# One message product per turn of sixteen tiles, in 256 columns, and both comparisons ahead of sixteen adds

## The chip, the core and the metric

The kernel runs on one core of one Trainium2 chip. The core has five engines: TensorE (PE in the rows, its weight loads PEld), VectorE (DVE), ScalarE (ACT), GpSimd (POOL) and SyncE (SP). The metric is the device time of one launch in microseconds (us). Lower is better.

## What is computed

Seven graph layers run over one graph of 6250 nodes and 106250 edges, each with source, destination, one of 8 relation types and a weight. Nodes have 128 features in float32. Five layers are relational and two are weighted means. The change touches the relational ones alone. Cut to what matters, one is

```python
hs = h[src]                                   # one row of 128 per edge
m = sum over b of coef[etype, b] * (hs @ bases[b])        # = hs @ W[etype]
agg = segment_sum(m, dst, num_segments=h.shape[0])
h = relu(agg + h @ loopw + bias) + h_prev
```

Edges come sorted by destination.

## The kernel before

**Tiles.** Edges are cut into 832 tiles of 128. Since destinations are sorted, the 128 edges of a tile fall into a window of 16 neighbouring nodes. A tile's 128 gathered source rows are multiplied on TensorE with a 128x128 table of zeros and ones (`onehot`), whose 128 columns are 8 relations by 16 nodes of the window. That gives, for each relation and each node of the window, the sum of its source rows. These sums then go through the 8 relation matrices, added up in PSUM, and give the messages of the 16 nodes. So weights are applied after the summing, once per window and not once per edge.

**Turns.** Sixteen tiles (`RING`) make a turn, in two halves of eight (`HALF`, h = 0 and 1), and each half in two quads (q = 0 to 3). A relational layer has 52 turns, five layers have 260. A turn, named k, does this:

- GpSimd (L500 to L509) issues 16 indirect DMAs, one per tile, that gather 128 rows of 512 bytes into the slots of `rows_in`. Eight slots of a half may be filled again once the sums of that half are done: it waits for `summed[1]` before half 0 and for `summed[3]` before half 1.
- VectorE (`turn`, L1020 to L1028) makes the tables. `onehots(h)` is 8 comparisons of 128x128 and waits until the sums of the same half in the turn before have read the old ones. `adds(h)` loads 8 window starts, waits for `messaged[h]`, and adds 8 blocks of 128x16 from PSUM into `acc`. Its order is onehots(1), adds(0), onehots(0) of the next turn, adds(1).
- TensorE (`messages`, L764 to L784) makes for half 0 the eight sums, four into bank SUM[0] and four into SUM[1], waits for their evacuation, and then multiplies with the eight relation matrices W into bank MSG[0], 8 tiles by 16 nodes = 128 columns. The same follows for half 1 into MSG[1]. A quad's bank is free when ScalarE has evacuated the quad before it in that bank. The message product of a half also waits until VectorE has added the half of the turn before (`added`).
- ScalarE (`evacuate`, L582 to L590) copies each quad's bank, 128x512, into `sums`.

An engine works its own instructions in program order. What connects them is semaphores: `gathered` (a DMA has landed), `onehot_ready`, `summed`, `evacuated`, `messaged`, `added`. Between turns stand the steps of a chunk of 512 nodes, 13 per layer, whose turns are all done: VectorE applies the relu and adds the old node values, TensorE transposes, and a layer with a normalisation adds moments and a scaling on VectorE. They are interleaved by `edge_chunks`, which runs the turns that a chunk needs and then one step of its pipeline.

Each float32 matmul of the program stands in the trace as two PE rows and two PEld rows, so x16 is eight matmuls.

## Time and profile before

| | |
|---|---|
| median of 3 runs | 9659.97 us (9652.16 to 9668.2) |
| the profiled execution | 9735.56 us, of which the span 9733.8 us |
| TensorE busy | 5450.5 us (56%) |
| VectorE busy | 3272.6 us (34%) |
| ScalarE busy | 1283.5 us (13%) |
| GpSimd busy | 6642.2 us (68%) |
| granted TensorE clock, mean | 0.668 of full speed |
| rows_in gathers of GpSimd | 4160, in five layers of 52 turns |

The page lists busy time of each engine, the span in 40 slices, DMA queues, the chain of work that ended last, and the costliest groups of instructions. An engine's idle time before a group is put down to what ended it. "remote" stands where the event that ended it is not followed back to one instruction, and "issue" where the engine waited for nothing that the profile shows.

### The profile page before, as it was taken

What the parts mean: (1) busy time and instruction counts of PE and PEld (TensorE: products, weight loads), DVE (VectorE), ACT (ScalarE), POOL (GpSimd) and SP (SyncE); (2) the same over time, 40 slices, a digit from 0 to 9 for tenths busy, and PEclk for the clock granted to TensorE, in tenths of its full rate; (3) what the DMA queues carried; (4) which work ended last, traced back from release to release, by engine and by line L of the source; (5) the groups of instructions that cost most, each with busy time, mean ns of one, the idle gap of its engine ahead of it and who ended that gap; (6) DMA issues with size and microseconds to landing.
All of it is one profiled execution on the core that took longest, in us unless ns stands there. A gap on an engine that the chain in (4) does not pass through costs nothing.

```text
span 9733.8 us, 121762 instructions
## 1 busy us (share of the span) xinstructions
PE 5450.5 (56%) x27756; PEld 4997.4 (51%) x27757; DVE 3272.6 (34%) x16373; ACT 1283.5 (13%) x3064; POOL 6642.2 (68%) x5897
## 2 busy tenths in 40 slices
PE   4444554544454455767767544445444546776775
PEld 4444444444444444666666444444444445666664
DVE  3332333333333333433333333333233334333333
ACT  1100111011101111111111200111101111111112
POOL 5666656666566665888888666665666666888887
PEclk7777777677767776555555677777777775555556
DMA  2222221111111111555555511111111114555556
GB/s 92 68 67 67 68 55 45 46 46 46 46 44 45 45 47 45 81 74 74 74 76 74 105 44 46 46 46 46 43 45 45 47 45 73 74 75 76 74 74 114
DMA packets 578875, 595.00 MB, mean 61 GB/s; under 512 B 128465, under 2 KB 470718, under 8 KB 578494
## 3 DMA queue, kind: packets, MB, share of 16 engines
q0 software_dynamic: 373312, 383.17, 23.9%
q1 hardware_dynamic: 170246, 190.65, 6.8%
q10 hardware_dynamic: 35192, 19.90, 0.6%
q14 instruction: 94, 0.77, 0.0%
q8 instruction: 31, 0.51, 0.0%
HBM read 431.39 MB, written 161.82 MB: 61 GB/s over the span
## 4 chain that ended last, share of the span: by engine, by line
another core or an unknown queue 39%; issue 17%; DMA 15%; POOL 13%; PE 8%; ACT 4%; DVE 2%; ACTq 2%; DVEq 1%; SPq 0%; POOLq 0%
DMA share<-scat,place 14%; POOL share L478 13%; PE msg L781 5%; ACT sums L587 4%; PE sum L774 2%; PE lin L726 1%; ACTq L125 1%; DVE acc L980 0%; DVE onehot L967 0%; ACTq L123 0%; ACTq L122 0%; DVE stats L1118 0%; DVEq L967 0%; PE lin L818 0%
## 5 line engine op out<-in xcount | busy, mean ns | idle before, releaser
L509 POOL DMA_INDIRECT rows_in<-h_table,edges_i x3328 | 3171.1, 953 | 1939.9 <-issue 1020.2
L478 POOL DMA_INDIRECT share<-scat,place x1664 | 2601.7, 1564 | 589.9 <-issue 312.8
L781 PE MATMUL msg<-sums,mix_w 128*128 128x128 f32 x4992 | 1137.0, 420 | 1865.8 <-ACT sums L587 1220.1
L781 PEld LDWEIGHTS msg<-sums,mix_w 128*128 128x128 f32 x4992 | 1054.6, 321 | 1927.4 <-issue 1643.1
L980 DVE TENSOR_TENSOR acc<-msg,acc 128x16 f32 x4160 | 729.6, 175 | 3805.3 <-issue 1262.4
L806 PE MATMUL msg<-rows_in,sums 16*128 16x128 f32 x3328 | 1267.4, 482 | 905.7 <-ACT sums L601 904.2
L781 PE MATMUL msg<-sums,rel_w 128*128 128x128 f32 x3328 | 757.0, 419 | 1248.4 <-ACT sums L587 712.7
L806 PEld LDWEIGHTS msg<-rows_in,sums 16*128 16x128 f32 x3328 | 880.7, 322 | 993.3 <-issue 505.8
L781 PEld LDWEIGHTS msg<-sums,rel_w 128*128 128x128 f32 x3328 | 703.6, 322 | 1287.5 <-issue 986.5
L967 DVE TENSOR_SCALAR onehot<-iota_ps,keyT 128x128 f32<-128x128 f32 x4160 | 1166.4, 345 | 477.8 <-issue 442.6
L774 PE MATMUL sum<-onehot,rows_in 128*128 128x128 f32 x8320 | 1262.1, 315 | 73.9 <-issue 46.8
L774 PEld LDWEIGHTS sum<-onehot,rows_in 128*128 128x128 f32 x8320 | 1246.0, 236 | 84.3 <-issue 52.1
L587 ACT ACTIVATE sums<-sum 128x512 f32<-128x512 f32 x1040 | 601.8, 596 | 5211.2 <-remote 3599.9
L509 POOL DMA_INDIRECT rows_in<-in_x_dram,edges_i x832 | 788.6, 948 | 494.7 <-issue 247.5
L808 PEld LDWEIGHTS lin<-ones,sums 16*128 16x128 f32 x3328 | 890.4, 324 | 0.0
L797 PE MATMUL sum<-onehot,near 128*16 128x128 f32 x3328 | 735.6, 415 | 2.5 <-DVE onehot L994 2.5
L808 PE MATMUL lin<-ones,sums 16*128 16x1 f32 x3328 | 693.3, 275 | 0.0
L1006 DVE SCALAR_TENSOR_TENSOR place_f<-repeats,to_spareT 128x8 f32<-128x8 f32 x208 | 35.0, 168 | 1847.1 <-ACT scat L611 1846.1
L797 PEld LDWEIGHTS sum<-onehot,near 128*16 128x16 f32 x3328 | 464.4, 145 | 186.7 <-DVE onehot L994 3.4
L994 DVE TENSOR_SCALAR onehot<-edges_i,srcT 128x128 f32<-128x128 int32 x1664 | 498.4, 312 | 0.0
L607 ACT ACTIVATE place<-place_f 128x4 int32<-128x4 f32 x416 | 85.5, 206 | 2525.9 <-POOLq L477 2511.9
L1000 DVE CUSTOM_DVE_ANT_0 mean<-onehot,before 128x128 f32<-128x128 f32 x1664 | 372.2, 289 | 7.2
(141 smaller groups left out, 2197.3 us busy)
## 6 DMA issues: line engine op xcount, KB each, us to landing
edges_i<-in_src_dram SPq DMA_DIRECT2D x210, 512.0 KB
rows_in<-h_table,edges_i POOLq DMA_INDIRECT x3328
share<-zeros SPq DMA_DIRECT2D x104, 258.0 KB
rows_in<-h_table SPq DMA_DIRECT2D x1664, 8.0 KB
share<-scat,place POOLq DMA_INDIRECT x1664
hT<-share SPq DMA_DIRECT2D x80, 258.0 KB, 4.9
h_table<-rows ACTq DMA_DIRECT2D x65, 256.0 KB
rows_in<-in_x_dram,edges_i POOLq DMA_INDIRECT x832
```

Source lines behind the costliest of these rows:

```text
L478: nc.gpsimd.indirect_dma_start(out=shares[m][a], out_offset=bass.IndirectOffsetOnAxis(ap=place[:, q // 2, 4 * (q % 2) + a:4 * (q % 2) + a ...
L509: nc.gpsimd.indirect_dma_start(out=rows_in[:, s, :], out_offset=None, in_=rows_of[:, :], in_offset=bass.IndirectOffsetOnAxis(ap=srcT_i[:, ...
L587: act.activation(sums[:, h, :, 4 * (q % 2):4 * (q % 2) + 4, :].rearrange("p r t v -> p t r v"), SUM[q % 2][:, :].rearrange("p (t r v) -> p ...
L774: last = nc.tensor.matmul(SUM[q % 2][:, t * KEYS:(t + 1) * KEYS], rows_in[:, 4 * q + t, :], onehot[:, 4 * q + t, :], start=True, stop=True)
L781: last = nc.tensor.matmul(MSG[h][:, 0:HALF * WIN], W[:, n, :], sums[:, h, n, :, :].rearrange("p t v -> p (t v)"), start=(n == 0), stop=(n ...
L797: last = nc.tensor.matmul(SUM[q % 2][0:WIN, t * D:(t + 1) * D], near[:, 4 * q + t, :], same[:, 4 * q + t, :], start=True, stop=True)
L806: nc.tensor.matmul(MSG[q % 2][:, t * D:(t + 1) * D], to_edges, win_rows[:, 4 * q + t, :], start=True, stop=True)
L808: last = nc.tensor.matmul(LIN[q % 2][:, t:t + 1], to_edges, ones[0:WIN, 0:1], start=True, stop=True)
L967: ins = nc.vector.tensor_scalar(onehot[:, slot, :], IOTA[:, 0:KEYS], keyT[:, bass.ds(i * RING + slot, 1)], None, ALU.is_equal)
L980: nc.vector.tensor_tensor(acc[:, at], MSG[h][:, s * WIN:(s + 1) * WIN], acc[:, at], ALU.add).then_inc(added, 1)
L994: ins = nc.vector.tensor_scalar(same[:, slot, :], src_all[:, h, s * D:(s + 1) * D], srcT[:, at], None, ALU.is_equal)
L1000: ins = nc.vector.tensor_tensor_reduce(out=unused[:, s, :], in0=same[:, HALF * h + s, :], in1=before[:, :], scale=1.0, scalar=0.0, op0=ALU ...
```

## The change

It has two parts, both in the turn of a relational layer.

- **One message product.** TensorE now makes the sums of all four quads first and then waits for all four evacuations and for all 16 adds of the turn before. Then it multiplies with the eight relation matrices once, 256 columns wide, into bank MSG[0] alone. `messaged` is one semaphore in place of two. ScalarE, whose evacuation of a half waited for the product of that half in the turn before, now waits for the one product of the turn before.
- **VectorE's order.** onehots(1), onehots(0) of the next turn, adds(0), adds(1). Both halves of adds wait for the one `messaged`, and the second reads columns 128 to 255 of MSG[0].

```diff
@@ scalar: evacuate
-                            act.wait_ge(messaged[h], k + 1)
+                            act.wait_ge(messaged, k + 1)
@@ tensor: start
-            for h in range(2):
-                pe.sem_inc(messaged[h], 1)
+            pe.sem_inc(messaged, 1)
@@ tensor: messages
                                 last.then_inc(summed[q], 1)
-                            for q in (2 * h, 2 * h + 1):
-                                pe.wait_ge(evacuated[q], k + 1 + h)
-                            pe.wait_ge(added, k * RING + HALF * h + HALF)
-                            for n in range(N_RELS):
-                                last = nc.tensor.matmul(MSG[h][:, 0:HALF * WIN], W[:, n, :],
-                                                        sums[:, h, n, :, :].rearrange("p t v -> p (t v)"),
-                                                        start=(n == 0), stop=(n == N_RELS - 1))
-                            last.then_inc(messaged[h], 1)
+                        for q in range(4):
+                            pe.wait_ge(evacuated[q], k + 1 + q // 2)
+                        pe.wait_ge(added, k * RING + RING)
+                        for n in range(N_RELS):
+                            last = nc.tensor.matmul(MSG[0][:, 0:RING * WIN], W[:, n, :],
+                                                    sums[:, :, n, :, :].rearrange("p h t v -> p h (t v)"),
+                                                    start=(n == 0), stop=(n == N_RELS - 1))
+                        last.then_inc(messaged, 1)
@@ vector: adds
-                    dve.wait_ge(messaged[h], k + 2)
+                    dve.wait_ge(messaged, k + 2)
...
-                        nc.vector.tensor_tensor(acc[:, at], MSG[h][:, s * WIN:(s + 1) * WIN], acc[:, at],
+                        nc.vector.tensor_tensor(acc[:, at], MSG[0][:, (HALF * h + s) * WIN:(HALF * h + s + 1) * WIN], acc[:, at],
@@ vector: turn
                         onehots(1, i, k)
-                        adds(0, i, k)
                         with dve.If(i < TURNS - 1):
                             onehots(0, nc.s_assert_within(i + 1, min_val=1, max_val=TURNS - 1,
                                                           skip_runtime_bounds_check_because="the condition above"), k + 1)
+                        adds(0, i, k)
                         adds(1, i, k)
```

TensorE's instructions of one turn stood so before (an x8 is eight matmuls of the program, ISA and REGISTER_ALU are the preparation of waits):

```order
L773 ISA
L774 MATMUL sum<-onehot,rows_in 128x128 x8
L779 ISA
L781 MATMUL msg<-sums,mix_w 128x128 x8
L774 MATMUL sum<-onehot,rows_in 128x128 x8
L778 REGISTER_ALU
L779 REGISTER_ALU
L781 MATMUL msg<-sums,mix_w 128x128 x8
```

and now stand so:

```order
L772 ISA
L773 MATMUL sum<-onehot,rows_in 128x128 x16
L777 REGISTER_ALU
L778 ISA
L780 MATMUL msg<-sums,mix_w 128x256 x8
```

The product of the first half is gone from between the two groups of sums, and the one at the end is twice as wide.

On VectorE, behind the last comparison of onehots(1), stood the loading of the window starts and the first add of half 0:

```order
L967 TENSOR_SCALAR onehot<-iota_ps,keyT 128x128
L973 ISA
L973 TENSOR_LOAD window
L976 REGISTER_ALU
L978 ISA
L980 ISA
L980 TENSOR_TENSOR acc<-msg,acc 128x16
```

and now stands the branch and the comparisons of the next turn's half 0:

```order
L966 TENSOR_SCALAR onehot<-iota_ps,keyT 128x128
L1022 COMPARE_AND_BRANCH
L963 REGISTER_ALU
L966 ISA
L966 TENSOR_SCALAR onehot<-iota_ps,keyT 128x128
```

The adds of half 0 moved behind those comparisons, directly ahead of the adds of half 1, where now stands, between the eighth and the ninth add:

```order
L979 TENSOR_TENSOR acc<-msg,acc 128x16
L972 REGISTER_ALU
L972 TENSOR_LOAD window
L977 REGISTER_ALU
L979 ISA
L979 TENSOR_TENSOR acc<-msg,acc 128x16
```

So all sixteen adds of a turn now stand in one piece, with one loading of window starts inside it.

## Rows read from the trace of the kernel before

**Rows 1.** The page's groups: line engine op, out<-in xcount | busy, mean ns | idle before, releaser.

```profile
L509 POOL DMA_INDIRECT rows_in<-h_table,edges_i x3328 | 3171.1, 953 | 1939.9 <-issue 1020.2
```

**Rows 2.** Groups by line of the stretch 1600 to 2500 us, same columns.

```profile
L509 POOL DMA_INDIRECT rows_in<-h_table,edges_i x597 | 566.2, 948 | 336.5 <-remote 175.1 <-issue 161.1 <-PE sum L774 0.3
L781 PE MATMUL msg<-sums,mix_w 128*128 128x128 f32 x1200 | 276.4, 423 | 448.4 <-ACT sums L587 320.5 <-issue 99.9 <-DVE acc L980 28.0
...
L774 PE MATMUL sum<-onehot,rows_in 128*128 128x128 f32 x1200 | 183.8, 317 | 5.3 <-issue 3.8 <-DMA rows_in<-h_table,edges_i 1.5
...
L967 DVE TENSOR_SCALAR onehot<-iota_ps,keyT 128x128 f32<-128x128 f32 x592 | 166.7, 345 | 71.2 <-issue 66.5
L980 DVE TENSOR_TENSOR acc<-msg,acc 128x16 f32 x599 | 105.1, 175 | 538.3 <-issue 256.6 <-PE msg L781 132.3 <-remote 79.9
```

**Rows 3.** The waits, 1600 to 2500 us: who for whom, us, times, longest.

```profile
ACT sums L587 <- remote: 514.2, 84, 17.4
...
POOL rows_in L509 <- remote: 175.1, 73, 3.9
POOL rows_in L509 <- issue: 161.1, 523, 1.9
```

**Rows 4.** Timeline, one half-turn: start us, us, engine line op, idle before.

```profile
3027.83 0.95 POOL L509 DMA_INDIRECT rows_in<-h_table,edges_i  x1 [2.78 <-remote]
...
3028.33 3.78 PE L781 MATMUL msg<-sums,mix_w 128*128 128x128 f32 x16 [6.21 <-ACT sums L587]
...
3031.89 2.60 PE L774 MATMUL sum<-onehot,rows_in 128*128 128x128 f32 x16
3032.34 2.32 DVE L980 TENSOR_TENSOR acc<-msg,acc 128x16 f32 x8 [2.60 <-PE msg L781]
...
3033.70 0.60 ACT L587 ACTIVATE sums<-sum 128x512 f32<-128x512 f32 x1 [5.61 <-PE sum L774]
...
3036.59 0.95 POOL L509 DMA_INDIRECT rows_in<-h_table,edges_i  x1 [0.30 <-issue]
3039.27 0.60 ACT L587 ACTIVATE sums<-sum 128x512 f32<-128x512 f32 x1 [4.97 <-remote]
3040.04 0.95 POOL L509 DMA_INDIRECT rows_in<-h_table,edges_i  x1 [2.50 <-remote]
...
3040.10 3.65 PE L781 MATMUL msg<-sums,mix_w 128*128 128x128 f32 x16 [5.61 <-ACT sums L587]
```

**Rows 5.** Timeline at the end of layer 1, where GpSimd falls silent after 2570.5 us.

```profile
2556.88 1.06 PE L818 MATMUL lin<-ident,y 128*128 128x128 f32 x4
...
2568.41 2.33 DVE L980 TENSOR_TENSOR acc<-msg,acc 128x16 f32 x8 [16.65 <-remote]
2568.96 1.57 POOL L522 DMA_INDIRECT share<-zeros,lane_i  x1 [0.31 <-issue]
2571.18 0.60 ACT L622 ACTIVATE rows<-lin 128x512 f32<-128x512 f32 x1 [18.10 <-remote]
...
2573.83 2.16 DVE L967 TENSOR_SCALAR onehot<-iota_ps,keyT 128x128 f32<-128x128 f32 x8 [1.47 <-issue]
...
2578.76 2.20 PE L774 MATMUL sum<-onehot,rows_in 128*128 128x128 f32 x16
...
2580.99 0.60 ACT L587 ACTIVATE sums<-sum 128x512 f32<-128x512 f32 x1 [0.23 <-PE sum L774]
```

**Rows 6.** Timeline of a turn in which GpSimd issued sixteen gathers without a pause.

```profile
1503.36 0.95 POOL L509 DMA_INDIRECT rows_in<-h_table,edges_i  x1 [2.65 <-remote]
...
1512.56 2.05 PE L781 MATMUL msg<-sums,mix_w 128*128 128x128 f32 x16 [3.13 <-issue]
...
1522.11 0.95 POOL L509 DMA_INDIRECT rows_in<-h_table,edges_i  x1 [0.30 <-issue]
1526.09 1.08 ACT L587 ACTIVATE sums<-sum 128x512 f32<-128x512 f32 x2 [13.77 <-remote]
...
1526.89 0.95 POOL L509 DMA_INDIRECT rows_in<-h_table,edges_i  x1 [3.83 <-remote]
```

**Rows 7.** Timeline: VectorE's chunk step of a layer with normalisation, first and last group.

```profile
3022.25 0.69 DVE L1102 SCALAR_TENSOR_TENSOR y<-acc,hT 128x512 f32<-128x512 f32 x1 [0.39 <-DVE acc L980]
...
3025.21 1.37 DVE L1144 TENSOR_SCALAR rows<-lin,mv,rstd 128x128 f32<-128x128 f32 x4 [0.15 <-issue]
```

More of the change, by code:

```diff
@@ L275, in build @@
         evacuated = [sem(f"evacuated{q}") for q in range(4)]
-        messaged = [sem(f"messaged{h}") for h in range(2)]
+        messaged = sem("messaged")
         added = sem("added")
```

## The prediction, made before the changed kernel had run

> **What bounds the kernel now.** Read the page's groups first. GpSimd's gathers are the largest, 3171.1 us busy and 1939.9 us idle before them over 3328 of them [rows 1]. That is 1.54 us per gather, 24.6 us per turn of 16, with what lies between layers in it. In a stretch inside a layer there are 597 gathers in 900 us, 1.508 us each, so a turn takes **24.12 us** and a half 12.06 [rows 2]. Of that a gather is 0.948 us busy, and 161.1 us over 523 times is 0.31 us that lies between two gathers whatever happens [rows 3]. Sixteen of them are 16 x 1.25 = 20.0 us. The other 4.1 us of a turn are waits put down to "remote": 175.1 us over 73 times, 2.4 us each, one per half. GpSimd waits there for the sums of the half whose slots it wants to fill.
>
> The timeline of one half shows who makes it wait [rows 4]. GpSimd starts its eight gathers at 3027.83 and issues the last at 3036.59. TensorE's message product runs 3028.33 to 3032.1, and then its eight sums to 3034.5. ScalarE evacuates the first quad at 3033.70, at once. It takes the second only at 3039.27, and GpSimd resumes at 3040.04, 12.21 us after it began. The second quad's sums are recorded as finished 4.8 us before anyone acts on them. No gather is missing: before the sums TensorE is idle for 5.3 us in all of the 900 us [rows 2]. The same shows in the waits, where ScalarE spends 514.2 us waiting for something that the trace can't follow back [rows 3].
>
> Where does that hold of some 5 us come from? Two places of the trace bear on it. At the end of layer 1 TensorE's transposes are recorded until 2557.9, while GpSimd keeps issuing until 2570.5. ScalarE takes their result at 2571.18, 13 us late, and VectorE's adds start at 2568.41 though the product ahead of those transposes was over before 2556.9. Then GpSimd is silent, and the next sums, recorded until 2580.96, are evacuated at 2580.99, with no delay at all [rows 5]. In the other place GpSimd issued 16 gathers from 1503.36 without a pause, the last at 1522.11, and the sums that TensorE had made long before were evacuated at 1526.09 [rows 6]. I read it so: while GpSimd issues gathers, a result of TensorE that comes late in the run of gathers is seen only when GpSimd pauses, and one that comes in the first 4 us of a run is seen at once, as the product is (ended 3032.1, adds at 3032.34 [rows 4]). Why, I can't say. If that is so, the bound is a loop of two: GpSimd pauses for the sums, and the sums are seen because it pauses.
>
> **The change, part by part.** All times below count from T, the moment at which the last quad of a half is seen. GpSimd starts 0.77 us after T (3039.27 to 3040.04) and ends a run of eight at about T + 10.5. The next T is at T + 12.1.
>
> *The product of half 0 goes.* Before, after T of half 0, TensorE did evacuation and start 0.83 us (3039.27 to 3040.10), product 3.65 us, sums 2.0 to 2.6 us: ready at T + 6.5 to 7.1, and held. Now the sums of half 1 need only the evacuations, 2 x 0.60, and 2.6 us: ready at T + 3.8. The 3.65 us are not a gain by themselves, for they lay beside GpSimd's 10 us of issuing. They decide only whether the result falls into the early part of the run.
>
> *The wide product.* At the lower clock the eight matmuls of 128 columns take 3.78 us [rows 4], at the high one 2.05 us [rows 6]. Twice the columns in as many instructions is 4.1 to 7.6 us. Below that, down to one times 2.05, nothing is likely, since the columns are what both numbers scale with. TensorE idles before it as before, so I take the low end of the clock for half of it, 5.9 us. It ends at T + 0.83 + 5.9 = T + 6.7 (4.9 to 8.4), and the sums of the next half 0 follow to T + 8.7 (6.9 to 11.0). Before, that was T + 6.5 to 7.1. Both are ahead of the next T at 12.1, so the 2 us cost nothing. If the hold were gone they would be on the path.
>
> *Halved weight loads.* Their rows overlap the matmuls. I cost them at nothing.
>
> *VectorE's order.* Adds are 2.33 us for eight [rows 5]. Sixteen are 4.7, and the loading of window starts between them about 0.8, since the sequencer can no longer do it behind comparisons (an estimate, half of the 1.47 us that VectorE shows as "issue" before comparisons in [rows 5], where it also went through a loop's end). Then onehots(1) of the next turn takes 2.16 us [rows 5]. Counted from the end of the product: 0.25 + 5.5 + 0.5 + 2.2 = 8.4 us, so T + 15.1 for a product ended at T + 6.7. The sums of half 1 need that table, and they can't start before the next T, T + 12.1, and its two evacuations, T + 13.3. So the table is up to 2 us late for them, they are ready 5 us after the next T, and that still is ahead of the one after it, at 12.1. A chunk step adds 4.3 us (3022.25 to 3026.58 [rows 7]): ready 9.3 us after T, still ahead. VectorE has 65 of these steps and they cost nothing, as long as the product is seen when it ends. New behind the wait for `messaged` are then the eight adds of half 0, onehots(1) and, behind these, the sums of half 1.
>
> *The sum.* With the hold as I read it, two pauses per turn stay and a turn stays at 24.1 us. A gain comes only in turns where the sums of half 1 are ready so early (T + 3.8) that GpSimd needs no pause before half 1. Such a turn lasted 1526.89 - 1503.36 = 23.53 us, 0.6 less [rows 6]. But in it the product then comes late in a run, at about T + 10, is seen only at the pause, and makes the following turn's half 1 late, so every second turn at most: 130 x 0.6 = 78 us. I take a third of the turns, 87 x 0.6 = 50 us, and set against it 30 us for turns in which table or product slip past the pause, an amount between 0 and 65 steps x 1.5 us = 100 us. Forecast: -20 us. The profiled execution is 9735.56 us and would be 9716. The median of the runs is 75.6 us lower, so **9640 us**. The case's own range is 9540 to 9760.
>
> **Rivals.** *The hold belongs to TensorE's sums and not to GpSimd's issuing.* Then it is a fixed 7.2 us from the end of the product to the second quad seen (3032.1 to 3039.27 [rows 4]), twice a turn, and the change takes one product and one evacuation from a chain: 7.2 + 0.6 + 7.2 + 0.8 + (4.1 to 7.6) = 19.9 to 23.4 us. GpSimd can't do a turn under 20.0 + 0.77 = 20.8. So 20.8 to 23.4 against 24.1, that is 180 to 860 us less: 8800 to 9480, middle 9200. For it: the 7.2 us recur in nearly all halves. Against it: in [rows 5] and [rows 6] the hold is 13 and 10 us where GpSimd issues longer, and nil where it is silent. The Trainium skill, SBUF — State Buffer, section "SBUF: two separate sides", says that engine ports and DMA ports can't contend and that TensorE's port waits for nobody. By that rule GpSimd's gathers would not delay sums and this rival would hold, 9200 us. The two places of the trace speak against that reading, but neither shows a port.
>
> *VectorE becomes the link (slower).* If the product, late in a run, is not seen when it ends but at the next pause, then 16 adds, the loading and onehots(1), 8.4 us, start only at T. The table is there at T + 8.4, the sums of half 1 at T + 9.4, at the edge of the run's end at 10.5. With the chunk step's 4.3 us [rows 7] it is T + 13.7. It decides from 12.1 on. That gives 1.6 us or 100 us for 65 steps, and a pause that stretches by up to 1.5 us in each turn gives up to 390 us more: 9760 to 10150, middle 9900. For it: the wide product ends 6 us into a run, where quads are held. Against it: the old product, 4 us in, is seen at once, and a pause ends any hold.
>
> *The change does nothing of what it says.* It removes a wait that lay beside GpSimd's issuing; exactly no effect is 9660, inside my own case.
>
> **Chances.** My case 0.5, the first rival 0.28, the slower rival 0.2, all else 0.02. A measurement of this kernel can tell about 0.2%, 19 us. My case gives 0.2 faster, 0.13 within and 0.17 slower, so with the rivals 0.48 faster, 0.14 same, 0.38 slower. The range must leave out 0.2: downward the deeper part of the first rival (below 9250, some 0.12), upward the tail of the slower one (above 9930, some 0.08).
>
> **What would show it.** In the profile after: GpSimd's waits for "remote" still once per half and about 2.4 us each if I am right, gone or halved if the first rival is. The product's group with 256 columns between 260 and 480 ns per instruction, and 16 of them between 4.1 and 7.6 us. The evacuation of the fourth quad within 1 us of its sums in turns where these are ready early. If instead TensorE's sums wait for comparisons (a releaser "DVE onehot" before them), the slower rival is at work. I am wrong if gathers come closer than 1.45 us on average inside a layer, or farther than 1.58.

## The result, and the profile after

The changed kernel takes **9742.6 us** (9737.57 to 9749.81, 4 runs) against 9660.0 us for the kernel before beside it (9652.16 to 9668.2, 4 runs). The ratio is 1.0089, 95% interval 1.0076 to 1.0101: slower by 0.9%. Forecast was 9640 us.

The changed kernel's groups of the stretch 1600 to 2500 us, in the columns of [rows 2]:

```profile
L509 POOL DMA_INDIRECT rows_in<-h_table,edges_i x598 | 564.2, 943 | 335.9 <-issue 164.5 <-remote 127.9 <-PE sum L773 43.5
L773 PE MATMUL sum<-onehot,rows_in 128*128 128x128 f32 x1202 | 215.5, 352 | 391.2 <-DVE onehot L966 198.9 <-issue 192.3
L780 PE MATMUL msg<-sums,mix_w 128*128 128x256 f32 x608 | 212.7, 525 | 83.5 <-ACT sums L587 42.6 <-issue 40.9
L979 DVE TENSOR_TENSOR acc<-msg,acc 128x16 f32 x595 | 104.3, 175 | 571.6 <-remote 265.2 <-issue 115.9 <-PE msg L780 100.5
```

and its waits in the same stretch (us in all, times, longest), to be laid beside [rows 3]:

```profile
DVE acc L979 <- remote: 265.2, 16, 17.4
ACT sums L587 <- remote: 244.6, 41, 16.2
PE sum L773 <- DVE onehot L966: 198.9, 20, 15.8
POOL rows_in L509 <- remote: 127.9, 48, 4.0
```

Inside a layer almost nothing moved in sum: 598 gathers in 900 us against 597 [rows 2]. But who waits is new. Before, ScalarE waited 84 times for something that can't be followed back [rows 3]. Now it does so 41 times, and in its place VectorE's adds wait 16 times, up to 17.4 us each. Behind them TensorE's sums, which before waited 5.3 us in all [rows 2], wait 198.9 us for comparisons. A PE row of the product (each matmul has two) takes 525 ns with 256 columns against 423 with 128 [rows 2], and the product's busy time falls from 276.4 to 212.7 us, so one product costs less of TensorE than two, and that bought nothing. Another 192.3 us of idle time before the sums have no releaser that the profile shows.

The timeline shows one such turn:

```profile
3117.26 0.94 POOL L509 DMA_INDIRECT rows_in<-h_table,edges_i  x1 [2.43 <-remote]
...
3126.55 6.32 PE L780 MATMUL msg<-sums,mix_w 128*128 128x256 f32 x16 [2.78 <-issue]
...
3135.98 0.94 POOL L509 DMA_INDIRECT rows_in<-h_table,edges_i  x1 [0.30 <-issue]
3140.02 2.33 DVE L979 TENSOR_TENSOR acc<-msg,acc 128x16 f32 x8 [16.99 <-remote]
...
3143.10 2.33 DVE L979 TENSOR_TENSOR acc<-msg,acc 128x16 f32 x8 [0.75 <-DVE acc L979]
...
3151.05 4.23 DVE L966 TENSOR_SCALAR onehot<-iota_ps,keyT 128x128 f32<-128x128 f32 x16 [0.62 <-issue]
3152.23 3.71 PE L773 MATMUL sum<-onehot,rows_in 128*128 128x128 f32 x16 [16.70 <-DVE onehot L966]
...
3155.97 0.60 ACT L587 ACTIVATE sums<-sum 128x512 f32<-128x512 f32 x1 [0.98 <-PE sum L773]
3156.74 0.95 POOL L509 DMA_INDIRECT rows_in<-h_table,edges_i  x1 [5.93 <-PE sum L773]
```

GpSimd issues 16 gathers without a pause. The product is recorded as ended at 3132.87, 15.6 us into that run, and VectorE starts its adds only at 3140.02, when GpSimd has been silent for 3.1 us. Sixteen adds, a chunk step and the comparisons then stand ahead of the next sums, and GpSimd waits 5.9 us. It is the slower rival's mechanism. The gain is there too: the 16 gathers up to the next one, at 3140.89, took 23.63 us. Inside the layers the two roughly cancel.

The trace also records the signals themselves, the updates of the semaphores, apart from the matmuls. For this turn, in us:

| TensorE's work | recorded end | its signal |
|---|---|---|
| product | 3132.86 | 3139.80 |
| transposes of the chunk step, first group | 3133.30 | 3139.85 |
| transposes, second group | 3133.74 | 3139.91 |
| sums of the next turn, first quad | 3134.63 | 3140.01 |
| sums, second quad | 3135.52 | 3140.10 |

Five results whose recorded ends lie 2.66 us apart are signalled within 0.30 us. VectorE's adds start at 3140.02, and at 3140.03 ScalarE copies the second group of transposes. A quad's sums take 0.89 us by the records and these two signals are 0.09 us apart, so the second quad can't have been computed between them: the signals were held, and not all of the work was late. In after_again (below) the same shows in 166 halves whose two quads are both signalled over 1 us late: recorded ends 0.89 us apart in the median, signals 0.09. In before_again and after_fourth, where nothing is held, the recorded signals of sums and products stand at most 0.02 us behind the recorded end. Where results are held a part of the signals has no record (96 of 261 for the product in after_again), so these counts are lower bounds.

### The profile page after: what moved, and what is told of

The parts are those of the page before. It is cut to its first block and busy times, and to the rows that moved or that the text cites. A ratio compares the mean times of both kernels' runs of the same rounds, so it can differ in the third digit from the quotient of the medians.

```text
span 9742.1 us, 113436 instructions
## 1 busy us (share of the span) xinstructions
PE 5249.1 (54%) x23596; PEld 4530.9 (47%) x23597; DVE 3225.1 (33%) x16373; ACT 1286.5 (13%) x3064; POOL 6630.3 (68%) x5897
## 5 line engine op out<-in xcount | busy, mean ns | idle before, releaser
L509 POOL DMA_INDIRECT rows_in<-h_table,edges_i x3328 | 3164.0, 951 | 1959.4 <-issue 1060.6
L773 PE MATMUL sum<-onehot,rows_in 128*128 128x128 f32 x8320 | 1493.5, 352 | 2834.5 <-DVE onehot L966 1707.8
L773 PEld LDWEIGHTS sum<-onehot,rows_in 128*128 128x128 f32 x8320 | 1403.7, 260 | 2909.7 <-DVE onehot L966 1741.8
L966 DVE TENSOR_SCALAR onehot<-iota_ps,keyT 128x128 f32<-128x128 f32 x4160 | 1116.1, 343 | 402.1 <-issue 369.7
L509 POOL DMA_INDIRECT rows_in<-in_x_dram,edges_i x832 | 786.9, 946 | 481.3 <-issue 248.0
L780 PE MATMUL msg<-sums,mix_w 128*128 128x256 f32 x2496 | 843.6, 511 | 338.0 <-ACT sums L587 188.4
L780 PEld LDWEIGHTS msg<-sums,mix_w 128*128 128x128 f32 x2496 | 649.0, 267 | 513.5 <-issue 380.8
L780 PE MATMUL msg<-sums,rel_w 128*128 128x256 f32 x1664 | 570.5, 517 | 218.0 <-ACT sums L587 133.4
L780 PEld LDWEIGHTS msg<-sums,rel_w 128*128 128x128 f32 x1664 | 438.4, 270 | 337.1 <-issue 246.2
```

Of the source, the lines that this page charges most:

```text
L509: nc.gpsimd.indirect_dma_start(out=rows_in[:, s, :], out_offset=None, in_=rows_of[:, :], in_offset=bass.IndirectOffsetOnAxis(ap=srcT_i[:, ...
L773: last = nc.tensor.matmul(SUM[q % 2][:, t * KEYS:(t + 1) * KEYS], rows_in[:, 4 * q + t, :], onehot[:, 4 * q + t, :], start=True, stop=True)
L780: last = nc.tensor.matmul(MSG[0][:, 0:RING * WIN], W[:, n, :], sums[:, :, n, :, :].rearrange("p h t v -> p h (t v)"), start=(n == 0), stop ...
L966: ins = nc.vector.tensor_scalar(onehot[:, slot, :], IOTA[:, 0:KEYS], keyT[:, bass.ds(i * RING + slot, 1)], None, ALU.is_equal)
```

## Where the time went: the ends of the layers

Three sums over the five relational layers, worked out from the first and last L509 gather of each layer and its last add, in each profile. The rest of the span, all that lies outside these two sums, is the same within 10 us in all.

| profile (us) | span | first to last gather | last gather to last add | rest |
|---|---|---|---|---|
| order_only | 9656.6 | 6230.7 | 80.4 | 3345.5 |
| after | 9742.1 | 6261.3 | 131.3 | 3349.5 |
| before_profile | 9722.7 | 6297.3 | 79.0 | 3346.4 |
| after_again | 9798.7 | 6307.0 | 138.6 | 3353.1 |
| before_again | 8630.9 | 5225.8 | 54.5 | 3350.6 |
| after_fourth | 8665.9 | 5232.2 | 80.1 | 3353.6 |

Lines two by two are the kernel before (order_only is within 0.1% of it) and the changed one. The first and the last pair each come from two different sets of runs. The profile that the prediction reads isn't among them: it lies 75.6 us above the median of its own kernel (6289.1 between gathers, 94.9 in tails, 3349.8 rest). The middle pair was profiled in one set: of 76 us, **59.6 lie in five tails**, between a layer's last gather and its last add, 9.7 in all 260 turns, and 6.7 in the rest. The tail of the second layer in before_profile:

```profile
2572.15 1.57 POOL L522 DMA_INDIRECT share<-zeros,lane_i  x1 [0.30 <-issue]
2572.33 2.33 DVE L980 TENSOR_TENSOR acc<-msg,acc 128x16 f32 x8 [17.93 <-remote]
...
2577.71 2.16 DVE L967 TENSOR_SCALAR onehot<-iota_ps,keyT 128x128 f32<-128x128 f32 x8 [1.44 <-issue]
...
2581.96 2.91 PE L774 MATMUL sum<-onehot,rows_in 128*128 128x128 f32 x16
...
2588.00 2.32 DVE L980 TENSOR_TENSOR acc<-msg,acc 128x16 f32 x8 [3.28 <-PE msg L781]
...
2597.13 1.17 POOL L509 DMA_INDIRECT rows_in<-h_table,edges_i  x1 [23.41 <-issue]
```

and in after_again:

```profile
2570.52 1.57 POOL L522 DMA_INDIRECT share<-zeros,lane_i  x1 [0.30 <-issue]
2572.70 2.32 DVE L979 TENSOR_TENSOR acc<-msg,acc 128x16 f32 x8 [22.44 <-remote]
...
2575.97 2.32 DVE L979 TENSOR_TENSOR acc<-msg,acc 128x16 f32 x8 [0.95 <-DVE acc L979]
...
2581.36 2.16 DVE L966 TENSOR_SCALAR onehot<-iota_ps,keyT 128x128 f32<-128x128 f32 x8 [1.46 <-issue]
...
2582.54 3.78 PE L773 MATMUL sum<-onehot,rows_in 128*128 128x128 f32 x16 [22.34 <-DVE onehot L966]
...
2591.15 2.32 DVE L979 TENSOR_TENSOR acc<-msg,acc 128x16 f32 x8 [7.63 <-PE msg L780]
...
2594.23 2.32 DVE L979 TENSOR_TENSOR acc<-msg,acc 128x16 f32 x8 [0.76 <-DVE acc L979]
...
2603.73 1.05 POOL L509 DMA_INDIRECT rows_in<-h_table,edges_i  x1 [31.65 <-issue]
```

GpSimd has nothing left to issue here, so every step behind 2570 is on the path. From GpSimd's last issue to the next layer's first gather it is 23.4 us before and 31.7 us after. In it stand sixteen adds in place of eight, twice: once ahead of the comparisons, once at the end.

The tails also show held products. In after_again the last product but one had its recorded end 5.3 to 6.7 us ahead of the end of the layer's last gather in all five layers. In three of them its adds began only 3.1 to 8.2 us behind that gather, and behind them the last comparisons, at 11.4 to 16.8 us. In the other two layers these began at 6.1 and 8.5, and in before_profile at 2.4 to 3.6 in four layers of five.

A rival is the clock. TensorE's mean granted clock is lower in the changed kernel, 0.645 against 0.671 in the middle pair. But after_early (below) has the same 0.645 and is faster than the kernel before in its set, and in the last pair the clock falls as much, 0.669 to 0.642, for 35 us. The lower clock alone isn't the loss.

## Experiments

Runs of one set were on one chip, beside the kernel before. That kernel itself took 9654.1 us in set A, 8635.0 in B, 9725.6 in C, 9732.0 in D and 8639.3 in E, so times are compared inside a set alone.

### Set A: each part by itself

**order_only** is the kernel before with VectorE's new order and the two products as they were.

```diff
                         onehots(1, i, k)
-                        adds(0, i, k)
                         with dve.If(i < TURNS - 1):
                             onehots(0, ..., k + 1)
+                        adds(0, i, k)
                         adds(1, i, k)
```

> VectorE makes both tables ahead of the sixteen adds, and TensorE still makes two products of 128 columns. If the order is what costs (table of half 1 behind sixteen adds, so that its sums wait for it), this is as slow as the whole change or slower, 9700 to 9760 us: the adds of half 0 now wait behind onehots(0), which waits for summed[1] of the turn, and that is ahead of them anyway. If the wide product is what costs, this is within 20 us of 9660.

9662.4 us, ratio 1.0007 (0.9998 to 1.0016). The order costs and gives nothing.

**product_only** is the changed kernel with VectorE's old order, adds(0) ahead of onehots(0).

> One product of 256 columns, with VectorE's old order: onehots(0) of the next turn stand between the adds of half 0 and half 1, so they too come only after the product. If the order of the change costs, this is worse still, since now both tables come after the product: the sums of half 0 then can't start before the product is seen, 2.3 + 2.2 us later. Expected 9800 to 10200 us. If only the width of the product costs, this is as the whole change, 9740 us.

10266.4 us, ratio 1.0623 (1.0604 to 1.0642). It was expected at 9800 to 10200. Every table of half 0 now stands behind adds that wait for the product of the whole turn. Its waits, 1600 to 2500 us:

```profile
PE sum L773 <- DVE onehot L966: 287.1, 60, 13.4
```

So the change needs its second part, which wins back most of this and not all: onehots(1) of the next turn stays behind the wide product.

**after_early** takes that away too. Both tables of the next turn are made ahead of the sixteen adds.

```diff
-                        onehots(1, i, k)
-                        with dve.If(i < TURNS - 1):
-                            onehots(0, ..., k + 1)
+                        ahead(0)        # onehots(0) of the next turn
+                        ahead(1)        # onehots(1) of the next turn
                         adds(0, i, k)
                         adds(1, i, k)
```

The first turn's two tables are made ahead of the loop.

> The changed kernel, with onehots(1) of the next turn also made ahead of the sixteen adds, so that no sums wait for a table that stands behind adds. If the wait of the sums of half 1 for their table (some 1700 us of idle in the profile after) is what takes the gain away, each turn can run as the short ones, 23.0 to 23.5 us against 24.0, and the time is 9500 to 9620 us. If GpSimd's pauses set the pace whatever the others do, it stays within 40 us of 9660.

9615.8 us, ratio 0.9957 (0.9944 to 0.9971), faster than both kernels in this set. Its median turn is 23.58 us, with one pause of GpSimd per turn: 264 pauses, against 394 in the changed kernel and 495 in order_only. Its tails are 110.1 us, 30 above order_only's. Its product is acted on over 1 us late in 245 of 260 turns, and here that costs nothing, since no table stands behind the adds. So in this set late tables are what the changed kernel loses inside the layers, 6261.3 us between gathers against 6143.7, and the wider tail stays. Set D does not repeat it (below).

**half_gathers** is the kernel before with four of each half's eight gathers left out; both quads read the same four slots.

> The kernel before, in which GpSimd gathers only four tiles for each half and both quads are summed from the same four slots: half of the gathers is left out, all else is issued as before. GpSimd's run is then 5 us in place of 10. If sums are held because GpSimd is issuing, they are seen about 2 us after the run of four, or at once, and a half takes 7 to 8.5 us: relational layers of 750 to 900 us in place of 1250. If the hold is a fixed time of TensorE's sums (7.2 us from the end of a product), a half stays at 12.0 us and the layers at 1250.

6959.4 us. A half takes 6.65 us in the median and a layer 691 to 717, less than the lowest that was expected, and far from the 12.0 and 1250 of a fixed hold. A run of gathers in it:

```profile
2004.93 0.94 POOL L509 DMA_INDIRECT rows_in<-h_table,edges_i  x1 [1.94 <-PE sum L774]
...
2006.91 1.95 PE L774 MATMUL sum<-onehot,rows_in 128*128 128x128 f32 x16
...
2008.67 0.95 POOL L509 DMA_INDIRECT rows_in<-h_table,edges_i  x1 [0.30 <-issue]
...
2010.71 1.08 ACT L587 ACTIVATE sums<-sum 128x512 f32<-128x512 f32 x2 [5.96 <-remote]
2011.53 0.95 POOL L509 DMA_INDIRECT rows_in<-h_table,edges_i  x1 [1.91 <-remote]
```

The sums are recorded as done at 2008.86 and taken 1.1 us after GpSimd's last issue ended, at 2009.62. Before, with a run of eight, they were taken 4.8 us late and 1.7 us after the last issue [rows 4]. With the shorter run the delay is shorter.

### Set B: no hold at all

**before_again** is the kernel before, unchanged.

> The kernel before, unchanged, for a profile that lies nearer the median of its runs than the 9735.56 us one: 9650 to 9670 us. If the hold behind TensorE's sums is as I read it, GpSimd's pauses are once per half and 2.0 to 2.5 us long, and what the first profile had more lies in these pauses.

8632.7 us, where 9650 to 9670 was expected. Its groups of the stretch 1600 to 2500 us:

```profile
L509 POOL DMA_INDIRECT rows_in<-h_table,edges_i x705 | 668.3, 948 | 224.9 <-issue 221.2 <-PE sum L774 3.7
L774 PE MATMUL sum<-onehot,rows_in 128*128 128x128 f32 x1409 | 301.3, 342 | 200.6 <-DMA rows_in<-h_table,edges_i 196.3 <-DVE onehot L967 1.8 <-issue 1.5
```

GpSimd never pauses for "remote": 705 gathers in 900 us, a layer's end among them, against 597 [rows 2]. The median turn is 20.0 us, which is the 16 x 1.25 of the prediction. Sums wait for landing rows, and a result that ends in the middle of 52 turns of issuing is taken at once. The same program, then, meets the hold in some sets and in others not, and the hold is worth 1000 us.

**before_early** is the kernel before with both tables half a turn earlier: onehots(0) of the next turn, adds(0), onehots(1) of the next turn, adds(1).

> The kernel before (two products of 128 columns) with VectorE's order onehots(0) of the next turn, adds(0), onehots(1) of the next turn, adds(1). If the gain of the changed kernel with early tables comes from the tables alone, it is here too, 9600 to 9630 us. If it comes from the sums of half 1 following those of half 0 early in a run, so that GpSimd runs sixteen gathers and pauses once, the product of half 0 still stands between, the pauses stay two per turn, and the time is within 20 us of the kernel before.

8635.0 us, ratio 0.9999 (0.999 to 1.0008). Here, where GpSimd's issuing is the bound, this order costs nothing. What it does where results are held, which was the question, isn't answered.

**one_gather** is the kernel before with one gather per half in place of eight, seven left out, and all tiles of a half reading one slot. It ran here and again in set D.

> The kernel before with one gather per half, from which all eight sums are made: 7 of 8 gathers are left out. GpSimd issues for 1.25 us and is silent otherwise. If the hold comes from its issuing, every quad is evacuated within 0.3 us of its sums, and a half takes what the chain of engines takes: evacuation and start 0.83, product 2.0 (the clock stays up), sums 2.0, so 5 to 6 us. If it comes from TensorE's sums, the 5 us of delay are still there and a half takes 10 us or more.

6142.7 us, 4.9 us a half in the median, a little under the 5 to 6 expected. As nothing is held in this set, only the run in set D tells where the hold comes from.

### Set C: width, place and a pause, with the hold

**after_again** is the changed kernel.

> The changed kernel once more, beside before on the same chip. Theory: its loss comes from results that are held while GpSimd issues, and from the ends of the layers. On a chip where before takes 9655 us with turns of 24 us it takes 9735 to 9750, ratio 1.008 to 1.010. On a chip where before takes 8635 us with turns of 20 us nothing is held inside a layer: the turns tie at sixteen gathers of 1.25 us, and only the ends of the five layers are left, where product, sixteen adds and the last sums lie open: 5 x 3 to 5 x 10 us, so 8650 to 8685. Rival: the wide product and the sixteen adds are slow by themselves. Then the chip without a hold shows the same 85 us, 8720.

9801.4 us, ratio 1.0076 (1.0062 to 1.009). **before_profile**, the kernel before, took 9724.5 us in its one run and gave the third line of the table above.

**split_product** has two products of 128 columns at the end of the turn, in the place of the wide one.

```diff
-                        for n in range(N_RELS):
-                            last = nc.tensor.matmul(MSG[0][:, 0:RING * WIN], ...)
+                        for h in range(2):
+                            for n in range(N_RELS):
+                                last = nc.tensor.matmul(MSG[0][:, 128 * h:128 * h + 128], ...)
```

> The changed kernel with one edit: where the one product of 256 columns stood, at the end of the turn and behind all four evacuations, stand two of 128 columns, one behind the other, with one signal at the end. It tells the width from the place. Theory: what costs is the place (one product late, then sixteen adds in one piece), not the width; two products take 7.3 to 7.6 us at the lower clock against 6.7 for the wide one, both end inside the run of gathers and are seen at its end, so the time is within 0.2% of the changed kernel on either kind of chip. Rival: the width itself costs or gains; then it moves by 260 x 0.7 = 180 us.

9924.3 us, ratio 1.0202 (1.0186 to 1.0217), 123 us above the changed kernel. A miss: first to last gather takes 6429.4 us against 6307.0, 0.47 us more per turn, though the product lies beside GpSimd's issuing. But the run does not isolate the product's length, for by the records two products take hardly longer than the wide one: 5.46 us against 5.40 in the median, 5.43 against 5.21 on average, where 0.6 to 0.9 us more had been expected. What differs is the number of matmuls, and when the product is seen. Of 260 products 200 are followed by adds more than 1 us late, against 128 in after_again. Of those that ended 5 to 8 us into a run of gathers it is 73 of 113, against 14 of 107. So two products in place of one are seen later and cost 123 us; why, and what length alone would cost here, isn't shown.

The 128 of after_again sort by when the product ended in its run of gathers (counted from the trace):

| product ended, us into the run | products | adds over 1 us late |
|---|---|---|
| under 4 | 30 | 0 |
| 5 to 8 | 107 | 14 |
| 8 to 10 | 8 | 4 |
| 10 and more | 110 | 110, by 8.6 us on average |
| in silence, a layer's last | 5 | 0 |

Of the 128 late adds 105 started with GpSimd silent, after 3.05 us of silence in the median, and 23 while it was still issuing; in split_product it is 77 of 200 while issuing. So "seen only when GpSimd pauses" describes most cases and not all.

**mid_pause** is the changed kernel with one wait more, for the product of the turn before, after five gathers of the second half.

```diff
                             for s in range(HALF * h, HALF * (h + 1)):
+                                if s == HALF + 5:
+                                    pool.wait_ge(messaged, k + (i + 1))
```

> The changed kernel, with one wait more: GpSimd, five gathers into the second half of a turn, waits for the product of the turn before, and then issues the other three. Theory, on a chip with the hold: the product, recorded as ended at that point, becomes visible within 1 to 2.5 us of the silence, so VectorE's adds start there in every turn, not at the end of a run of gathers. Each turn pays a pause of about 2 us, and gets the tables earlier; 9900 to 10250 us. Rival: a product is visible a fixed 7 us or so after it ended, whatever GpSimd does. Then GpSimd stands still for those 7 us in each turn, 10900 us or more. On a chip without the hold both say that the wait costs what the product is late by, 0 to 2 us a turn: 8640 to 9150.

9722.9 us, 78.5 under the changed kernel and level with before. The time was missed, since I had priced the pause as an addition. The mechanism shows, in most turns and not in all (101 of 260 adds are still over 1 us late, against 128):

```profile
3094.42 5.90 PE L783 MATMUL msg<-sums,mix_w 128*128 128x256 f32 x16 [0.92 <-ACT sums L590]
...
3102.60 0.94 POOL L512 DMA_INDIRECT rows_in<-h_table,edges_i  x1 [0.30 <-issue]
3106.24 1.09 ACT L590 ACTIVATE sums<-sum 128x512 f32<-128x512 f32 x2 [12.10 <-remote]
3106.29 2.33 DVE L982 TENSOR_TENSOR acc<-msg,acc 128x16 f32 x8 [13.52 <-remote]
3106.86 0.94 POOL L512 DMA_INDIRECT rows_in<-h_table,edges_i  x1 [3.33 <-remote]
```

The product ended at 3100.32 and nobody acted on it for 6 us. 2.7 us after GpSimd fell silent the adds and two evacuations started, within 0.05 us of each other. All pauses of GpSimd sum to 1187 us against 1199 in after_again, so the extra silence is paid for by less at the ends of the runs. Of the gain, 39 us lie between first and last gathers (6268.0 us) and 29 in the tails (109.8).

### Set D: once more, timed

**after_third** is the changed kernel.

> The changed kernel a third time. What is open is its share on a chip without the hold. Theory by now: of its loss of 76 to 85 us, 52 to 60 lie between a layer's last gather and its last add (13 to 24 us before, 23 to 32 after, in five layers), the rest inside the layers. About 5.5 us of each tail is bare work, one wider product and eight more adds, and the others are tables that come late because results were held. So on a chip where before takes 8635 us only the bare work is left: 8635 + 5 x 3 to 5 x 6.5 us, 8650 to 8668, ratio 1.002 to 1.004; on a chip with the hold 1.007 to 1.010. Rival: the wide product and the sixteen adds are too slow in every turn. Then the ratio is near 1.008 on both kinds.

9813.6 us, ratio 1.0085 (1.0069 to 1.01), with tails of 139.7 us. Results were held again, so its question of a set without the hold waited for set E.

**mid_pause_timed** is mid_pause.

> The changed kernel with GpSimd's extra wait in the middle of the second half of a turn. Theory: on a chip with the hold the silence lets the product be seen 2 to 2.5 us after it starts, the sixteen adds and the tables behind them come in time, and this pays for the pause: within 0.2% of before, 0.7 to 0.9% under the changed kernel. On a chip without the hold the extra wait can only cost: the product ends 1 to 3 us after the fifth gather's issue in most turns, so up to 260 x 2 us, 8650 to 9200. Rival: the single look at it was luck; then it is as slow as the changed kernel, ratio 1.008.

9746.4 us, ratio 1.0013 (1.0004 to 1.0022): the extra wait wins back 67 of 82 us, as expected. The single run of set C was no luck.

**after_early_again** is after_early.

> The changed kernel with onehots(1) of the next turn, too, made ahead of the sixteen adds, so that no table stands behind the product. Theory: on a chip with the hold one pause per turn in place of two, turns of 23.6 us, ratio 0.994 to 0.997 as before. On a chip without the hold nothing is to be gained inside the layers, and the bare work of the five tails stays: 8645 to 8665, ratio 1.001 to 1.0035. Rival: the gain was of that one chip; then the ratio is 1.000 or above on a chip with the hold too.

9773.3 us, ratio 1.0041 (1.0027 to 1.0055). In set A it was 0.9957, so this is a miss, and the expectation's rival was right. No version here beats the kernel before in each set. Against after_third its tails are 22.8 us shorter, but between gathers it takes 6310.3 us against 6315.7: inside the layers the gain of set A is gone. In A 226 of its 264 pauses last 3.5 to 4 us; here 128 of 269 last 4 to 4.5, and all of them 1173 us against 1008. GpSimd's pauses for the same program, then, are longer in one set than in the other.

**one_gather_again** is one_gather, here in a set with the hold.

> The kernel before with one gather per half in place of eight, all eight tiles of a half read the same slot: seven of eight gathers are left out. It took 6143 us on a chip without the hold, where GpSimd is silent 88% of the time. Theory, the hold comes from GpSimd's issuing: with GpSimd silent nearly all the time there is nothing to hold, and a chip that takes 9655 to 9725 us for before takes 6130 to 6200 us here, the same as the other chip. Rival, the hold is a slower TensorE, PSUM or ScalarE path of that chip, whatever GpSimd does: then some 1000 us or 11% more here as well, 6700 or above.

6147.0 us, within 0.1% of the 6142.7 of set B, while the kernel before takes 9732 here and 8635 there. No signal of a sum or product is over 1 us late in either. (GpSimd is silent for some 82% of the relational layers there, not 88%.) So TensorE, PSUM and ScalarE are no slower here, and what costs 1000 us appears only beside GpSimd's gathers. The Trainium skill, SBUF — State Buffer, section "SBUF: two separate sides", says that engine ports and DMA ports can't contend and that TensorE and ScalarE wait for nobody. No record here shows a port. What these runs show is that TensorE's signals come late beside GpSimd's gathers (110 of 110 in the last group of set C's table). Whether a port has a part in that stays open.

### Set E: the changed kernel without the hold

**after_fourth** is the changed kernel.

> The changed kernel on one more chip. On a chip with the hold (before 9650 to 9730 us) ratio 1.007 to 1.010, with 50 to 65 us of it between the layers' last gathers and their last adds. On a chip without it (before 8635 us) the wider product and the eight more adds in five tails are all that is left: 8650 to 8668. Rival: a cost of the wide product in every turn, which gives near 1.008 on either.

8667.8 us, ratio 1.0032 (1.0019 to 1.0044). First to last gather is 5232.2 us against before_again's 5225.8, and the tails 80.1 against 54.5. Of 260 products none is seen late. What is left is 5.1 us a tail, the bare work of a wider product and eight more adds: the last product takes 5.3 us on average against 3.8, and from the last half's first add to the end it is 5.4 us against 2.3 in four of the five layers.

**short_product** (set B) and **short_product_again** are the changed kernel with six of the eight relations left out of the product.

> The changed kernel with the product cut to two of the eight relations (six are left out): it takes 1.5 us in place of 5.4 to 6. It tells what the length of the product costs where results are held. Theory: the product is the last result that has to be seen ahead of the adds and the tables; one that ends in the first 5 us of a run of gathers is seen at once, a later one not before the pause. The short one is always early, so adds and tables are in time in each turn: turns of 23.6 to 23.9 us and no sums of half 1 behind comparisons but those with chunk steps, 9600 to 9720 us on a chip where the changed kernel takes 9740 to 9810. Rival: the length lies beside GpSimd's issuing and is free, as the prediction had it; then only the tails get shorter, 5 x 4 us, 20 us under the changed kernel. On a chip without the hold 8645 us, as it was.

8645.4 and 8652.6 us, the latter 7.6 us above the 8645 expected, with ratio 1.0014 (1.0003 to 1.0024) and tails of 61.6 us: 3.7 us a tail less, about the time that the product lost. Both runs fell into sets without the hold. For the one in set B I had expected 9560 to 9630 with it; neither could test that.

## Why the prediction was wrong, point by point

- **What bounds the kernel: right.** Sixteen gathers of 1.25 us and two pauses of 2.4. Without the hold the turn is 20.0 us, and mid_pause and half_gathers show results seen when GpSimd falls silent. That the work was done before is shown by signals that come in one burst. The rule was drawn too sharply: 23 of 128 late adds started while GpSimd was still issuing.
- **The sum left out a term, the ends of the layers.** It counted 260 turns and no end of a layer. Cover was named for every piece of work, GpSimd's issuing, and never asked where that cover ends. [rows 5] shows such an end, with every step of VectorE in the open. Five tails cost 51 to 60 us with the hold. Of these 26 are bare work, since they stay without the hold; that the others are tables late behind held adds is read from the tails of after_again and fits mid_pause, which takes 29 us out of the tails. The forecast of -20 with that term would have been +31 to +40. It is the larger of the two steps that failed; the other is the price of the slips, two points below.
- **The wide product, "the 2 us cost nothing": wrong at the layers' ends, open inside them.** Its size was right, 5.4 us in the median and 6.3 in the turn shown against 5.9, though a PE row of it took 525 ns where at most 480 was forecast. In a tail it is on the path: short_product_again saves 3.7 us a tail. Inside the layers 93 of the 107 products that ended 5 to 8 us into a run were seen in time, and no run here lengthens the product alone.
- **VectorE's order, "as long as the product is seen when it ends": the condition failed,** in 128 turns of 260 (after_again). The sum did allow for it, in every second turn at most, and priced it at 30 us with 100 as its upper bound. Inside the layers the change costs 10 to 31 us in place of the -20 of the sum. If the gain is taken at its forecast 50, the slips cost 60 to 81 us (an estimate), two to three times the 30 of the sum. The price in the rival, 8.4 us from the product seen to the table, fits: from 3140.02 to 3153.2, where the eighth comparison ends, less the 4.4 us of a chunk step, is 8.8 us.
- **The gain of 50 us: seen alone in one set of two.** In set A after_early has turns of 23.58 us, and first to last gather is 87 us shorter than in order_only, more than the 78 that the sum had as its most. In set D it is not there.
- **The signs named in advance** fit this. TensorE's sums wait 198.9 us for comparisons, the sign of the slower rival. Gathers come at 1.505 us on average in the stretch, inside 1.45 to 1.58, and so told nothing of the loss. That sign looked inside a layer, and most of the loss lay at its end.
- **The first rival** (a hold that belongs to the sums, 9200) is out: one_gather_again shows no hold. **The slower rival** was right in mechanism and put at 9900. It was too high, since the late turns alternate with turns of 23.6 us: GpSimd's pauses inside the layers became fewer and longer, 396 against 504, and their sum did not grow (1199 us against 1236, after_again and before_profile). It had no tails either. The miss is therefore one of both accounts, the case's and the rival's.

## What to carry to other kernels

Work that hides beside a long-issuing engine is free only while that engine issues: count the ends of loops and layers apart, with nothing hidden, five times whatever stands there. When two batches are merged to save an instruction, what grows is the last one, which nothing covers, and every step queued behind its result on other engines. Where a result must be seen during another engine's long run, a deliberate short wait there can cost less than it gives: here it won back 67 of 82 us, and no more than that.

## What was not expected of the hardware

- One and the same program takes 9654 to 9732 us in some sets and 8635 to 8639 in others, 11% less. The difference is GpSimd's pauses: inside the layers 504 of 2.45 us on average in before_profile, 1 in before_again. The records name the same chip for set A and for set E, so it may be no property of a chip. What sets it stays open.
- TensorE's signals can come late in bursts while its work is done, up to 13 to 14 us behind the recorded end of sums in after_again, and at most 0.02 us where nothing is held. Products that end 10 us or more into a run of gathers were seen late in 110 cases of 110 in after_again, by 8.6 us on average, and in none in after_fourth.
- A PE row of an fp32 product of 256 columns takes 525 ns where one of 128 takes 423. Halving the instructions took 23% off the product's busy time on TensorE (276.4 to 212.7 us in 900 us), and nothing off the kernel's time.
